# First attention of a four-stage kernel: units of four sequences by half instead of blocks of two sequences, and halves at the ends of the routed stages

## What is computed

```python
def attn(x, W_qkv, b_qkv, W_out, b_out, w_sur, b_sur, threshold):   # 16 heads of 16
    spikes = (sigmoid(x @ w_sur + b_sur) > threshold)
    q, k, v = split(x @ W_qkv + b_qkv)
    tq, sq = expmap0_split(q); tk, sk = expmap0_split(k)    # cosh, sinh(.)*u/norm
    neg_inner = tq tk^T - sq sk^T
    dist = arccosh(max(neg_inner, 1 + 1e-7))
    scores = where(causal, -dist**2 / sqrt(16), -inf)
    y = (softmax(scores) * spikes) @ v
    return y @ W_out + b_out
# typed: per sequence one of 5 experts, relu(x @ wi[e]) @ wo[e]
# moe:   per token one of 4 experts, (silu(g) * u) @ proj[e], [g, u] = h @ wv[e]
```

## Time and profile before

| | us |
|---|---|
| median of 3 runs (2227.09 to 2229.27) | 2228.93 |
| profiled execution | 2227.89 |
| its span | 2226.1 |
| `hyp_in`, from the table load to the last spike step | 1199.26 to 1261.01 |
| first attention's loop, first `stretch` to last `add` | 1262.04 to 1405.18 |
| `typed`, first to last matmul | 1607.02 to 1754.9 |
| last `y_row` of `moe` starts | 2217.39 |

### The profile page before, as it was taken

One profiled execution on the slowest core, in us unless ns is written; L12 is line 12 of the kernel. 1 busy time (PEld: TensorE's weight loads), 2 busy tenths in 40 slices (PEclk: granted clock), 3 DMA queues, 4 the chain that ended last, 5 costly groups with the idle time before them and its releaser, 6 DMA issues. The chain is left out here.

```text
span 2226.1 us, 32462 instructions
## 1 busy us (share of the span) xinstructions
PE 2035.3 (91%) x11700; PEld 1717.9 (77%) x11700; DVE 1106.0 (50%) x1946; ACT 935.9 (42%) x1916; POOL 720.6 (32%) x777
## 2 busy tenths in 40 slices
PE   7999999999999999999998767799899765968998
PEld 6888888888888888888887545678699734858998
DVE  3334433443343344344344787333377574856775
ACT  4242323324233232323323599322255354645664
POOL 3030200203021020302200198202178314868884
PEclk9999999999999999999999798999999877978999
DMA  4010010101001010110000200320056303446661
GB/s 162 1 57 1 1 57 0 57 0 51 6 0 57 0 57 0 39 43 0 1 1 19 67 31 37 117 76 10 0 182 208 103 16 109 172 165 214 211 216 55
DMA packets 97922, 144.50 MB, mean 65 GB/s; under 512 B 15567, under 2 KB 72817, under 8 KB 97841
## 3 DMA queue, kind: packets, MB, share of 16 engines
q1 hardware_dynamic: 90784, 127.42, 17.7%
q0 software_dynamic: 4928, 12.86, 1.6%
q10 hardware_dynamic: 2128, 3.15, 0.4%
HBM read 109.32 MB, written 12.06 MB: 55 GB/s over the span
## 5 line engine op out<-in xcount | busy, mean ns | idle before, releaser
L584 DVE TENSOR_TENSOR cond_h<-cond_silu,ps 128x512 f32<-128x512 f32 x288 | 198.1, 688 | 696.5 <-ACT cond_silu L495 693.1
L495 ACT ACTIVATE cond_silu<-ps 128x512 f32<-128x512 f32 x288 | 172.3, 598 | 771.7 <-PE ps L414 771.7
L414 PE MATMUL ps<-a_x_hi,cond_w_hi 128*128 128x512 f32 x1152 | 449.3, 390 | 2.0 <-DVE a_x_lo L262 2.0
L414 PE MATMUL ps<-a_x_lo,cond_w_hi 128*128 128x512 f32 x1152 | 448.9, 390 | 0.0
L414 PE MATMUL ps<-a_x_hi,cond_w_lo 128*128 128x512 f32 x1152 | 448.7, 390 | 0.0
L383 POOL TENSOR_TENSOR cond_w_lo<-cond_stage_up,cond_w_hi 128x256 fp32r<-128x256 f32 x144 | 108.6, 772 | 832.3 <-ACT cond_w_hi L476 832.3
L414 PEld LDWEIGHTS ps<-a_x_hi,cond_w_hi 128*128 128x128 f32 x1152 | 216.7, 188 | 47.3 <-DVE a_x_lo L262 2.4
L414 PEld LDWEIGHTS ps<-a_x_hi,cond_w_lo 128*128 128x128 f32 x1152 | 216.6, 188 | 45.2
L414 PEld LDWEIGHTS ps<-a_x_lo,cond_w_hi 128*128 128x128 f32 x1152 | 216.7, 188 | 44.9
L430 PE MATMUL ps<-cond_h_hi,cond_d_hi 128*128 128x512 f32 x576 | 224.5, 390 | 3.4 <-DVE cond_h_lo L552 3.4
L430 PE MATMUL ps<-cond_h_hi,cond_d_lo 128*128 128x512 f32 x576 | 224.1, 389 | 0.0
(11 more groups left out here) (369 smaller groups left out, 4105.4 us busy)
## 6 DMA issues: line engine op xcount, KB each, us to landing
moe_stage_up<-in_L_ffn_expert_wv SPq DMA_DIRECT2D x22, 1024.0 KB, 8.2
typed_stage_up<-in_L_cond_wi SPq DMA_DIRECT2D x11, 1024.0 KB, 4.9
typed_stage_dn<-in_L_cond_wo SPq DMA_DIRECT2D x11, 1024.0 KB, 5.9
moe_stage_dn<-in_L_ffn_expert_proj SPq DMA_DIRECT2D x11, 1024.0 KB, 6.8
cond_stage_up<-in_L_cond_Wg SPq DMA_DIRECT2D x7, 1024.0 KB, 4.8
cond_stage_up<-in_L_cond_Wu SPq DMA_DIRECT2D x7, 1024.0 KB, 6.8
cond_stage_dn<-in_L_cond_Wd SPq DMA_DIRECT2D x7, 1024.0 KB, 5.4
hyp_v_now<-hyp_v_blk SPq DMA_DIRECT2D x16, 272.0 KB, 2.3
```

The source lines that it names most:

```text
L414: ins = pe.matmul(up_ps[st % 2][j], w[:, j, k, fs], x[:, k, tok], start=(i == 0), stop=(i == 3 * KC - 1))
L495: act.activation(silu[:, st % 2], up_ps[st % 2][0], ACT.Silu).then_inc(act_done, 1)
L584: dve.tensor_tensor(h[:, st % 2], silu[:, st % 2], up_ps[st % 2][1], ALU.mult).then_inc(up_free, 1)
```

## The change

The part of the first attention behind `hyp_in` becomes a function of its own, `hyper_units`, in which a unit is four sequences and one half of their queries: unit n = 2i is the first 32 queries of four sequences, with 32 keys ("light" below, 512 elements of a row), unit 2i + 1 their last 32 queries with all 64 keys ("heavy", 1024 elements). There are 16 units. q and k are made by blocks as before, and both blocks of a pair must be there for its first unit. `score` is 16 matmuls of 32 queries, `mix` 32 matmuls of 32 queries, straight from v_blk; v_now and its transfers go. The first half of `prob`'s buffer is cleared once, so that `p_turn`, `p_take` and `mix` stay full. `y_take` goes to VectorE. All iterations are written out, lags and orders are new. The spike sums become 128 matmuls of 32 tokens. The table load moves behind two `round_src`. In `typed` (LoadLate) x_hi comes behind two w_hi, and x_lo is VectorE's first. In both routed stages `nought` moves behind the w_hi, and in the last slot the halves have banks of their own, no `nought` matmul, two `y_row` and a send behind each.

```diff
+def hyper_units(nc, m, tag, resT, qk, v_blk, space, spike, wo, bo):
...
+    keys = (S, T)
+    causal = [m.const[:, at:at + n].unsqueeze(1).to_broadcast([P, H, n]) for at, n in zip((C_FIRST, C_SECOND), keys)]
+    lag = dict(turn=1, q_blk=1, k_blk=2, score=3, clamp=3, root_sq=3, root_ln=4, root=4, root_add=4, dist_ln=4,
+               dist=5, mask=5, top=6, shift=5, prob=6, p_turn=7, p_take=7, mix=8, y=8, y_turn=8, y_take=9, out=9,
+               add=9, stretch=1)
+    order = dict(tensor='out mix score p_turn y_turn turn',
+                 scalar='root_ln dist root p_take prob q_blk root_sq dist_ln',
+                 vector='y_take k_blk add top stretch y clamp', gpsimd='mask root_add shift')
+    last = max(lag.values())
...
+            for it in range(NP + last):
+                for ph in order[name].split():
+                    if 0 <= it - lag[ph] < NP:
+                        phases[ph](it - lag[ph], (it - lag[ph]) % 2)
...
+                def score(n, q):
+                    pe.wait_ge(q_taken, n // 2 * 2 + 2)
+                    pe.wait_ge(k_blocked, n // 2 * 2 + 2)
+                    wait(pe, clamped, n)
+                    for c in range(KC):
+                        for r in range(2):
+                            for sq in range(4):
+                                buf, j = (n // 2 * 2 + sq // 2) % 4, sq % 2
+                                feat, h = slice(r * T, (r + 1) * T), c * GH
+                                asked = slice(j * T + q * S, j * T + (q + 1) * S)
+                                ins = pe.matmul(s_ps[q][sq * S:(sq + 1) * S, r, h:h + GH], qT[feat, buf, c, asked],
+                                                k_blk[feat, buf, c, j, :, 0:keys[q]], start=True, stop=True)
+                    ins.then_inc(scored, 1)
...
+                def mix(n, q):
+                    pe.wait_ge(p_taken, n + 1)
+                    wait(pe, y_scaled, n)
+                    for hp in range(HP):
+                        for sq in range(4):
+                            row = slice(sq * S, (sq + 1) * S)
+                            ins = pe.matmul(y_ps[row, hp * 2 * VW:(hp + 1) * 2 * VW], pT[:, q, hp, row],
+                                            v_blk[:, n // 2 * 2 + sq // 2, sq % 2, hp].rearrange("p h v -> p (h v)"),
+                                            start=True, stop=True)
+                    ins.then_inc(mixed, 1)
...
+                def root_square(n, q):
+                    act.wait_ge(clamped, n + 1)
+                    wait(act, masked, n - 1)
+                    act.activation(wide(t, q), wide(z, q), ACT.Square).then_inc(root_squared, 1)
...
+                def dist_log(n, q):
+                    act.wait_ge(root_added, n + 1)
+                    act.activation(wide(t, q), wide(z, q), ACT.Ln).then_inc(dist_logged, 1)
...
+                def stretch(i, q):
+                    wait(dve, turned, i - 1)
+                    dve.tensor_tensor(x[:, q].rearrange("p (h d) -> p h d", d=DH), qk[:, i].rearrange("p (h d) -> p h d", d=DH),
+                                      space[:, i].unsqueeze(2).to_broadcast([P, 2 * H, DH]), ALU.mult).then_inc(stretched, 1)
...
+                def clamp(n, q):
+                    dve.wait_ge(scored, n + 1)
+                    wait(dve, dist_logged, n - 1)
+                    dve.tensor_scalar(halves(z[:, q, 0:H * keys[q]].rearrange("p (a n) -> p a n", a=2), q), s_ps[q], float(np.float32(1.0 + 1e-7)), None, ALU.max).then_inc(clamped, 1)
...
+                def mask(n, q):
+                    pool.wait_ge(dist_done, n + 1)
+                    wait(pool, prob_done, n - 1)
+                    pool.tensor_tensor(wide(u, q), causal[q], wide(t, q), ALU.subtract).then_inc(masked, 1)
...
                         for i in range(NP):
-                            for k in range(KC):
-                                ins = pe.matmul(m.bank[7][:, i:i + 1], srcT[:, k, i * P:(i + 1) * P], ws[:, k:k + 1],
-                                                start=(k == 0), stop=(k == KC - 1))
+                            for sq in range(4):
+                                row, token = sq * T // 2, (i // 2 * 4 + sq) * T + i % 2 * T // 2
+                                for k in range(KC):
+                                    ins = pe.matmul(m.bank[7][row:row + T // 2, i:i + 1], srcT[:, k, token:token + T // 2], ws[:, k:k + 1],
+                                                    start=(k == 0), stop=(k == KC - 1))
                         ins.then_inc(spiked, 1)
...
                 def _(act):
-                    if hyper:
-                        act.preload_act_table_set("natural_log_exp_and_others")
-
...
                     round_src(1)
                     if hyper:
+                        act.preload_act_table_set("natural_log_exp_and_others")
...
+        if hyper:
+            hyper_units(nc, m, tag, resT, qk, v_blk, space, spike, wo, bo)
+            return
...
+                    if is_last(s):
+                        for i in range(HALVES):
+                            down_half(f, q, i)
+                        return
                     if f == 0:
+                        if is_first(s):
+                            pe.wait_ge(nought_made, 1)
                         pe.matmul(y_ps[q], nought[:, 0:P], nought[:], start=True, stop=False)
...
+                def down_half(f, q, i):
+                    for k, (x, w) in enumerate(((h_hi, d_hi), (h_lo, d_hi), (h_hi, d_lo))):
+                        ins = pe.matmul(y_last(q, i), x[:, f % HB, i * P:(i + 1) * P], w[:, f],
+                                        start=(f == 0 and k == 0), stop=(f == FC - 1 and k == 2))
+                    if f == FC - 1:
+                        ins.then_inc(dn_half_done, 1)
...
-                for f in range(FC - LAG, FC):
-                    dn_step(n - 1, f, (n - 1) % 2)
+                for i in range(HALVES):
+                    for f in range(FC - LAG, FC):
+                        if i == 0:
+                            pe.wait_ge(dn_ready, FC * (n - 1) + f + 1)
+                            pe.wait_ge(h_ready, FC * (n - 1) + f + 1 + UB)
+                        down_half(f, (n - 1) % 2, i)
...
-                act.activation(nought[:], m.zero_row[0:1].unsqueeze(1).to_broadcast([1, HALVES, D]), ACT.Copy)
-                for f in range(FC):
+                before_rows = 2 if prelude.rows_first else FC
+                for f in range(before_rows):
                     round_up(0, 0, 0, f)
+                if prelude.rows_first:
+                    round_x(0, 0)
+                for f in range(before_rows, FC):
+                    round_up(0, 0, 0, f)
+                act.activation(nought[:], m.zero_row[0:1].unsqueeze(1).to_broadcast([1, HALVES, D]), ACT.Copy)\
+                    .then_inc(nought_made, 1)
                 for f in range(0, DN, 2):
                     round_dn(0, 0, 0, f)
-                round_x(0, 0)
+                if not prelude.rows_first:
+                    round_x(0, 0)
...
+                if prelude.rows_first:
+                    split_x(0, 0)
                 for f in range(DN):
                     round_dn(0, 0, 0, f)
-                split_x(0, 0)
+                if not prelude.rows_first:
+                    split_x(0, 0)
...
+                    for i in range(HALVES):
+                        dve.wait_ge(dn_half_done, i + 1)
+                        if carried:
+                            dve.tensor_tensor(y_row[:, q, i], y_last(q, i), keep[:, q, i], ALU.add).then_inc(y_taken, 1)
+                        else:
+                            dve.tensor_copy(y_row[:, q, i], y_last(q, i)).then_inc(y_taken, 1)
```

171 lines of the change are left out of this document (167 added, 4 removed).

## The result

The changed kernel takes 2194.68 us (median of 4 runs, 2192.65 to 2199.83), the kernel before in the same comparison 2229.10 us (4 runs): a ratio of 0.9848, with a 95% interval of 0.983 to 0.9865. The profiled execution of after took 2196.37 us, its span 2194.6.

The account below looks back on a forecast made before the run. The prediction took the first attention's loop as bound by a ring through several engines; loop -17.6, spikes +7.4, table load -1.3, typed start -5, ends -1.4 and -1.7 sum to -19.6 from 2228.93, giving 2209 us (range 2198 to 2231).

Parts of the forecast that it names:

- the ring: First attention's loop: dist, mask, root_add, dist_ln, root_ln in turn set the pace, 6.3 us per unit against 7.67.
- filling and emptying: Start and end of the first attention's loop: 20.4 us before, 24.7 us after the change.
- the spike sums: Before the first attention's loop: the small matmuls take 21.3 us instead of 11.4, partly covered, 7.4 us more.
- The wait for the second block: Filling of the first attention's loop: the first score waits for a second block, 2.6 us more.
- The clock in the tail: End of the first attention's loop: longer mix and a fallen clock, 1.7 us more.
- The rival that had them covered: Before the first attention's loop: spike sums fully covered, their 7.4 us drop out, 2202 us; chance 17%.
- `score` and `mix`: TensorE in the first attention's loop: mix 1.1 us more, score unchanged, 5.7 to 6.3 us per unit.
- the second rival: First attention's loop: TensorE becomes the bound at full clock, 6.9 us per unit, 2219 us; chance 10%.
- the case of the half clock in the loop: First attention: TensorE at half clock, 10.6 us per unit; 2244 us with four pairs, 2278 with eight; chance 11%.
- Table load: Start of the first attention's hyp_in: ACT_TABLE_LOAD moves behind two roundings, 1.3 us less.
- `typed`: Start of the routed stage typed: x_hi and x_lo come earlier, TensorE starts sooner, 5 us less.
- the ends: Last slots of typed and moe: sending by halves saves 1.7 us in typed and 1.4 us in moe.

Follow-up runs that it names:

- p_take_half: Changed kernel with p_take copying only the first half of the row in every unit; pair 11.77 us, loop 118.6 us, total 2197.9 us.
- mask_half: Changed kernel with mask handling only 8 of the 16 heads in every unit; pair 11.32 us, loop 112.1 us, total 2190.5 us.
- light_wide: Changed kernel with the light unit also working on 64 keys, so every step is 1024 wide; pair 15.00 us, loop 143.3 us, total 2223.9 us.
- warm_both: Changed kernel with extra TensorE matmuls ending both attentions' first parts and in early loop iterations; first loop 118.6 us, second attention's pipeline 82.8 us.

## Why the prediction was wrong

The forecast fell short by 14.8 us. Three of its terms account for more than that: the ring (6.6), filling and emptying (2.7) and the spike sums (7.4).

**The direction and the mechanism of the loop were right, its size was not.** The ring is what sets the pace (p_take_half, mask_half), ScalarE's own work is what comes next and is 11.3 us as counted (mask_half), and TensorE has time to spare. The term that was mis-sized is the ring: 12.6 us per pair forecast, 11.77 measured. By parts: I took a heavy `mask` at 2.39 us and so 2.33 to the next `root_add`, where it takes 2.00 and 1.96; a light one at 1.25 to the next, where it is 1.07; for `dist` to a heavy `mask` 1.21, where it is 1.12; and 0.3 us for a `shift` in the way, where it was 0.1. 0.83 x 8 = 6.6 us. `mask` is the largest part, and all 16 of it are of one size in the kernel before (first line) and of another in light_wide, where all are 1024 wide too (second line):

```profile
L1412 POOL TENSOR_TENSOR hyp_u<-const,hyp_t x16: 2374/2388/2403, 1276.2 to 1390.5; 128x1024 f32<-128x1024 f32 x16
```

```profile
L966 POOL TENSOR_TENSOR hyp_u<-const,hyp_t x16: 1995/2001/2007, 1279.7 to 1391.2; 128x1024 f32<-128x1024 f32 x16
```

What VectorE does beside it doesn't explain that: before, it is busy for 2.2 us beside a `mask` in the middle of the loop and for 0.7 beside each of the last two, and all take 2.38 or 2.39; in after it is busy for 1.8 beside a heavy one in the middle and for 0.6 beside the last, and both take 2.00. The new `mask` reads its constant from another place (C_SECOND instead of C_CAUSAL), and the tiles lie elsewhere; no run takes these apart, so the cause is open. No row of before could have told it.

**Filling and emptying** were forecast at 24.7 us behind the 16 units. By the same count they are 116.1 - 16 x 5.88 = 22.0, 2.7 us less, though not much more than the 20.4 of before. The wait for the second block (2.6 us) is there, but the light unit that comes first hides it by passing its steps faster: before, the first `dist_ln` came 12.0 us behind the first `stretch`, in light_wide 14.6, and in the changed kernel 11.8. The clock in the tail that I had priced at 1.7 us stood at 1.00 in after but for one short fall; in p_take_half, where it fell, it cost 2.5.

**The spike sums** were the largest single error: +7.4 us forecast, nothing measured. The step that failed is the price of a record of 32 rows, 52 ns at full clock and 91 at half, taken from a line through 128 and 64 rows. With changing quarters a record took 10 ns, so that 247 of 256 passed ahead of the fall of the clock, and even in one quarter it took only 32 and 51. The line's own point for 128 rows was misread too: the earlier trace rows counts records that reach into the stretch, and 178 ns is 11.37/64, a mean over both clocks; it is 112 at full clock and 213 at half. I had two rows for larger tiles and none for a change of quarters, and took the middle where the nearer row (`mix`, 60 ns at half clock for two parts) already gave a covered group. The rival that had them covered, at 17%, was the right one. The cover itself wasn't tried beyond what was known: the longest group of any run, 11.07 us, is shorter than the 11.37 of before.

**`score` and `mix`** were priced too high as well: 32 quarter-height `score` records pass in 1.09 us for a heavy unit and 0.67 for a light one, 64 `mix` records in 0.77 us, less than the 32 of before in 1.13. So the second rival (TensorE as the bound, 6.9 us per unit) is refuted, and the case of the half clock in the loop didn't come: the clock stood at 1.00 from 1292 to 1360.

**The smaller terms held.** Table load 1.3 us forecast, 1.3 at TensorE's start and about 1 in the stage; `typed` 5 forecast, 5.3 in the stage; the ends 1.7 and 1.4 forecast, 1.9 and 2.0. That v_now, the loop written out and the branches are worth nothing fits light_wide, which has them only in sum with the new order.

**Not forecast** was a loss of about 1.5 us in the first part of the second attention.

With the ring at 11.77, the fill at 22.0 and the spikes at nothing, the sum would have been -27.0 - 1.3 - 5 - 1.4 - 1.7 = -36.4, against -34.4 measured.

## What to carry to other kernels

A pace set by a ring through several engines scales with the widths of its own steps; adding up its parts start to start, heavy and light, gave the mechanism and missed the size by 7%, mostly through one GpSimd step that took 2.00 us in the new kernel and 2.39 in the old one at the same width, for a cause that stays open. Small stationary tiles are not priced by scaling larger ones: a record of 32 columns cost 0.29 of one of 128, and 0.09 where every fourth changed its part of the array. A count of records in a stretch has those at its edges in it. Before a short step is moved between queues, follow which queue waits for it and what stands ahead of it in its new place: with the same copy of 0.4 us in ScalarE's queue a pair took 20 us instead of 11.8.

## What the runs showed of the hardware

- Spike records (f32, one moving column), start to start: 112 ns with 128 weight columns, 32 with 32 in one quarter, 10 with 32 and changing quarters, all at 2.4 GHz; 213 and 51 ns for the first two at 1.2 GHz.
- On ScalarE, an instruction that reads the result of the one right ahead of it starts 0.13 us later than one that doesn't (1.09 against 0.96 us, 1.17 against 1.04, for 128x1024).
- GpSimd's `mask` of 128x1024 took 2.37 to 2.40 us in the old kernel and 1.99 to 2.01 in the new one, whatever VectorE did beside it. Its heavy `shift` took 2.28 us in the new kernel while a `stretch` ran beside it and 1.90 in the last units, where none is left. VectorE's `stretch` took 2.19 in the middle of the old loop, and 0.68 and 1.72 in turn in the new one.
- With extra matmuls the clock stood at 1.00 from 1265 to 1350 in warm_both (in after 0.50 until 1292, with one short exception); where the next real one stood behind them they cost their own time, four of 256 columns (eight records) 3.56 us at half clock.
